# Five tables of steps, one for each engine, in place of one common order in a decoder layer's last third

## The chip, the cores and the metric

The kernel runs on one core of one Trainium2 chip. The metric is the device time of one execution in microseconds (us), as the median of several executions. The core has five instruction queues that run side by side: TensorE (PE, matrix products), VectorE (DVE), ScalarE (ACT), GpSimd (POOL) and SyncE (SP, which here only starts transfers). Each queue is worked off strictly in the order in which it was written; between queues there are only semaphores.

## The reference

One pre-norm decoder layer over 16 sequences of 128 tokens with 256 channels. Three residual blocks follow each other:

```python
# latent attention, 16 heads, latent width 72, causal
Wdkv = x @ latent_w + latent_b
q = jnp.einsum('btc,hcl->bhtl', x, Wd_w) + Wd_b[None, :, None, :]
scores = jnp.einsum('bhtl,bsl->bhts', q, Wdkv) / jnp.asarray(np.sqrt(d_head), dtype=x.dtype)
attn = jax.nn.softmax(jnp.where(causal, scores, -jnp.inf), axis=-1)
y = jnp.einsum('bhts,bsl->bhtl', attn, Wdkv)
z @ out_w + out_b
# bidirectional RWKV with the context as key and value, gate from x
jax.nn.sigmoid(r) * (Af + Ab + cur * v) / (Bf + Bb + cur)
# mixture of experts: 8 experts, 2 for each token
h = jax.nn.silu(x @ w_gate[e].T) * (x @ w_up[e].T)
out = out + dense_w[:, e:e + 1] * (h @ w_down[e].T)
x = x + attn(layernorm(x)); x = x + xattn(layernorm(x), ctx, ctx); x = x + ffn(layernorm(x))
```

## The kernel before

**Two halves.** The first half, to about 361 us, is attention and RWKV. Attention is cut into 64 units (one sequence, four heads each). The second half is the expert stage. Each token is written into a list of its two experts, and the lists are cut into tiles: 16 big tiles (0 to 15) of 256 rows and 7 small ones (16 to 22) of 128 rows. Tiles 0 to 4 are planned from the first 12 sequences (groups 0 to 2 of four sequences) before attention ends; all others wait for the last group's routing (`phase(j)` is 1 from tile 5 on).

**The names of the steps**, as the tables have them. A unit n of attention is `S.n` (scores on PE L727 and L731, their maximum on DVE L1197, exponentials on ACT L983), `N.n` (reciprocal DVE L1201, scaling POOL L1593), `T.n` (transposition PE L739, copy ACT L988), `Y.n` (mixing PE L748, copy DVE L1212, packing by four transfers on SP L574). `O.b.i` is quarter i of sequence b's output projection (PE L776, for sequence 15 L761), `add` adds two sequences' results to x.

For a group's second and third normalisation and routing there are `bn`, `agg`, `rs` (POOL L1588), `nmb`, `xn` (ACT L950), `tx` (transpositions PE L686, copies ACT L961), `lg` (router scores PE L792), `r1` and `r2` (the two choices, DVE L1294 to L1306, and exponentials on ACT L1032), `r3` (ranks, PE L799 and L803, slots on DVE L1321 to L1325), `rw` (weights, DVE to L1332), `r4` (eight scatters of token numbers into the lists, POOL L1636), and `p1`, `p2`, `p3` (which expert and which rows each tile has, some 40 short DVE instructions, L1340 to L1435).

A tile j of the expert stage goes through:

- `ltk.j`: its token numbers TK, loaded by SP at L631 or L633 (tiles 0 to 2: `gtk`, POOL L1668). Tiles from 5 on wait for `p3` of the last group and for its scatters.
- `lxg.j`: rows gathered by POOL (L1650, two instructions in a big tile, one in a small one) into one of four buffers; gather j waits until PE has transposed tile j-4.
- `lw.j.k`: weights of 512 KB for gate, up and down (k = 0, 1, 2), SP L620 and, for the small tiles, L604 (tile 0: `gw`, POOL L1660). Each waits until the block that lay there before has been split.
- `sw.j.k`: that block split into two parts, ACT L1048 and then DVE L1132 (big tiles only).
- `tg.j`: rows transposed (PE L818, ACT L1056 or L1054, DVE L1132).
- `up.j.n`: half n of the gate and up products (PE L668 with outputs P; a small tile has one, L852), then `si` (Silu, ACT L1062), `hd` (product, DVE L1463 or L1456) and `sh` (split, ACT L1069 and DVE L1132).
- `dn.j`: the down product (PE L668 with outputs PO, 24 matmuls; in a small tile L861, 8), then a copy with the weight (`weigh`, ACT L1077) into Y, one of two buffers.
- `ao.j`: POOL adds Y to the output rows in HBM (L1677). It waits until the additions of `ao.j-1` have landed. `weigh` of tile j waits until those of `ao.j-2` have landed.

```python
po.wait_ge(s_acc, 16 * parts_before(j))        # add_out, ahead of L1677
ac.wait_ge(s_acc, 16 * parts_before(j - 1))    # weigh, ahead of L1077
```

**What sets the order.** `schedule()` makes one list ORDER of 1060 steps: the text STEPS, and from tile 10 on a loop. Every engine walks this same list and emits its own part of each step. So a step that is late in the list is late on all five queues. The semaphore counts are also taken from ORDER (`nth`, `before`).

Of the kernel before, what the change touches and what calls it, by code (L numbers as in the profile page):

```python
# [1770 lines left out]
```

## Time and profile before

| | us |
| --- | --- |
| median of 3 executions | 604.07 |
| the three | 602.4, 604.07, 605.44 |
| the profiled execution | 600.46 |
| its span, first to last instruction | 598.8 |
| PE busy | 520.2 (87%) |
| VectorE, ScalarE, GpSimd busy | 362.9, 329.9, 314.7 |

All rows are of the one profiled execution, whose own time is 600.46 us: its span and 1.7 us around it. It lies 3.6 us under the median. Times of rows count from the start of the span.

### The profile page before, as it was taken

To read this page: it belongs to the slowest core of one execution; us is meant where nothing else is said; L and a number is where in the kernel's file an instruction comes from. 1 tells how busy PE (TensorE), PEld (TensorE's weight loads), DVE (VectorE), ACT (ScalarE), POOL (GpSimd) and SP (SyncE) were. 2 spreads that over 40 slices of the span, in tenths; PEclk is the share of its full clock that TensorE was granted. 3 is DMA by queue.
4 is the path that set the end of the run, shared out by engine and by line. 5 is a ranking of instruction groups with operands and counts; after the bars stand their busy time and mean duration, and the time that the engine had idled before them with its cause. 6 is when DMAs were issued, how large, how long until landed. Compare 5 with 4: busy or idle time off the path is not lost.

```text
span 598.8 us, 10336 instructions
## 1 busy us (share of the span) xinstructions
PE 520.2 (87%) x3448; PEld 453.2 (76%) x3448; DVE 362.9 (61%) x740; ACT 329.9 (55%) x945; POOL 314.7 (53%) x277
## 2 busy tenths in 40 slices
...
DMA packets 53219, 76.82 MB, mean 128 GB/s; under 512 B 10173, under 2 KB 41662, under 8 KB 52838
## 3 DMA queue, kind: packets, MB, share of 16 engines
...
q10 hardware_dynamic: 804, 0.15, 0.1%
...
## 4 chain that ended last, share of the span: by engine, by line
PE 58%; DVE 9%; issue 9%; POOL 9%; DMA 7%; ACT 5%; SPq 2%; POOLq 0%; DVEq 0%; ACTq 0%
PE P L668 18%; PE PO L776 7%; PE P L731 6%; PE P L748 6%; PE PO L668 5%; PE P L739 3%; PE P L852 3%; POOL EB L1593 2%; DMA cxa<-xd,TK 2%; POOL cxa L1650 2%; ACT EB L983 2%; PE PO L861 2%; PE P L727 2%; PE P L686 1%; PE P L792 1%
## 5 line engine op out<-in xcount | busy, mean ns | idle before, releaser
L983 ACT ACTIVATE EB<-P,small 128x128 f32<-128x128 f32 x256 | 90.4, 369 | 74.7 <-DVE small L1197 64.6
L1593 POOL TENSOR_TENSOR EB<-EB,small 128x512 f32<-128x512 f32 x64 | 78.8, 1241 | 86.1 <-DVE small L1201 86.0
L668 PE MATMUL P<-GT,WF 128*128 128x256 f32 x768 | 101.9, 291 | 6.0 <-DVE GT L1132 2.6
L668 PEld LDWEIGHTS P<-GT,WF 128*128 128x128 f32 x768 | 97.4, 198 | 7.2 <-DVE GT L1132 3.1
L1677 POOL DMA_INDIRECT out<-Y,TK x39 | 65.8, 1687 | 65.2 <-DMA out<-Y,TK 29.2
L731 PEld LDWEIGHTS P<-KT,qT 72*128 72x128 f32 x512 | 69.8, 198 | 11.5 <-DMA qT<-qP 6.4
L748 PE MATMUL P<-PT,V 128*72 128x512 f32 x128 | 67.0, 605 | 9.7 <-ACT PT L988 8.2
L731 PE MATMUL P<-KT,qT 72*128 72x128 f32 x512 | 70.3, 282 | 5.1 <-DMA qT<-qP 5.1
L776 PE MATMUL PO<-Ow,zP 128*128 128x256 f32 x270 | 67.5, 390 | 2.7 <-DMA zP<-ZT 2.7
L1212 DVE COPY ZT<-P 72x512 f32<-72x512 f32 x64 | 43.3, 676 | 40.4 <-PE P L748 39.4
L776 PEld LDWEIGHTS PO<-Ow,zP 128*128 128x128 f32 x270 | 50.5, 195 | 15.9 <-issue 10.3
L1197 DVE TENSOR_REDUCE small<-P 128x4 f32<-128x512 f32 x64 | 43.3, 677 | 26.3 <-PE P L731 26.1
L1650 POOL DMA_INDIRECT cxa<-xd,TK x39 | 42.9, 1100 | 30.1 <-DMA TK<-xs 20.0
L668 PE MATMUL PO<-WF,HR 128*128 128x256 f32 x384 | 51.9, 294 | 4.5 <-issue 4.5
L988 ACT ACTIVATE PT<-P 128x512 f32<-128x512 f32 x64 | 38.8, 607 | 27.8 <-PE P L739 27.8
L668 PEld LDWEIGHTS PO<-WF,HR 128*128 128x128 f32 x384 | 49.9, 202 | 4.9 <-issue 4.9
L983 ACT ACTIVATION_READ_ACCUMULATOR EB<-P,small 128x1 f32 x256 | 52.9, 207 | 0.0
L1636 POOL DMA_INDIRECT xs<-TKS,SL x32 | 33.7, 1052 | 35.9 <-DVE TKS L1332 25.6
L739 PEld LDWEIGHTS P<-ident,EB 128*128 128x128 f32 x256 | 31.4, 144 | 22.1 <-issue 10.7
L739 PE MATMUL P<-ident,EB 128*128 128x128 f32 x256 | 39.9, 279 | 4.6 <-POOL EB L1593 4.5
L1077 ACT ACTIVATE Y<-PO,TK 128x256 f32<-128x256 f32 x39 | 16.7, 470 | 38.9 <-DMA out<-Y,TK 15.0
L976 ACT ACTIVATE qP<-P,small 128x256 f32<-128x256 f32 x72 | 30.9, 483 | 12.4 <-PE P L668 12.3
...
## 6 DMA issues: line engine op xcount, KB each, us to landing
...
```

Source lines behind the costliest of these rows:

```text
L668: r = e.matmul(o, lt(a), rt_(b), start=start and n == 0, stop=stop and n == 2, skip_group_check=skip)
L731: p = e.matmul(S[:, 128 * j:128 * j + 128], qT[k % 2][:, 4 * hq + j, c:c + 128], KT[g % 2][:, r:r + 128], start=False, stop=True, skip_gro ...
L739: p = e.transpose(PTB[:, 128 * j:128 * j + 128], EB[n % 3][:, j, :], ident[:, :])
L748: e.matmul(YB[0:L, :], V[g % 2][:, b % GB, :], PT[n % 2][:, :], start=True, stop=True).then_inc(s_Y, 1)
L776: p = e.matmul(o, zP[b // NB % 2][:, m, 128 * (b % NB):128 * (b % NB) + 128], Ow[:, m, :], start=m == 0, stop=m == NQ - 1)
L983: e.activation(EB[i][:, j, :], S[:, 128 * j:128 * j + 128], ACT.Exp, bias=NM[i][:, j:j + 1], accum_out=SM[i][:, j:j + 1]).then_inc(s_exp, 1)
L988: e.activation(PT[n % 2][:, :], PTB[:, :], ACT.Copy).then_inc(s_pt, 1)
L1197: e.tensor_reduce(NM[n % 3], SB[n % 2][:, :].rearrange("p (h s) -> p h s", h=4), AX.X, ALU.max, negate=True).then_inc(s_max, 1)
L1212: e.tensor_copy(ZT[buf][:, :, c:c + 128], YB[0:L, :].rearrange("p (h t) -> p h t", h=4)).then_inc(s_z, 1)
L1593: e.tensor_tensor(EB[i][:, :, :], EB[i][:, :, :], SM[i].unsqueeze(2).broadcast_to([128, 4, 128]), ALU.mult).then_inc(s_prob, 1)
L1650: e.indirect_dma_start(XG[i][:, a_, :], None, xd[0:(TN * 3 // 4, TN + 1)[phase(j)], :], bass.IndirectOffsetOnAxis(ap=TK[:, j, a_, 0:1].bit ...
L1677: e.indirect_dma_start(outr, bass.IndirectOffsetOnAxis(ap=TK[:, j, a_, 0:1].bitcast(i32), axis=0), Y[j % 2][:, a_, :], None, bounds_check= ...
```

## The change

Each engine gets a text of its own with its own steps: SYNC_STEPS, TENSOR_STEPS, VECTOR_STEPS, SCALAR_STEPS and GPSIMD_STEPS. ORDER remains, but only for counting semaphores. No instruction's work, tile or buffer changes. Up to the scores of unit 53 every engine's steps stand as before. From there on (VectorE from unit 54, PE and ScalarE from 55, SP from the store of group 2's rows) they stand in another order, which differs from engine to engine.

```diff
+SYNC_STEPS = """
...
+    lw.11.0 lw.10.2 lw.12.1 lw.12.0 lw.13.1 lw.13.0 lw.11.2 lw.14.1 ltk.18 lw.12.2 lw.14.0 ltk.19 ltk.20 lw.13.2 lw.14.2 lw.15.1 lw.17.1 ltk.21 ltk.22
+    lw.15.0 lw.17.0 lw.16.0 lw.16.1 lw.15.2 lw.16.2 lw.18.0 lw.17.2 lw.18.1 lw.19.1 lw.18.2 lw.19.2 lw.19.0 lw.20.0 lw.20.2 lw.20.1 lw.21.2 lw.21.1
...
+def steps_of(table):
+
+    return [(name, *map(int, a)) for name, *a in (w.split(".") for w in table.split())]
+
+
 def schedule():
 
-    order = [(name, *map(int, a)) for name, *a in (w.split(".") for w in STEPS.split())]
+    order = steps_of(STEPS)
...
-            for name, *a in ORDER:
+            for name, *a in steps_of(SYNC_STEPS):
...
-            for name, *a in ORDER:
+            for name, *a in steps_of(TENSOR_STEPS):
...
-            for name, *a in ORDER:
+            for name, *a in steps_of(SCALAR_STEPS):
...
-                ve_.wait_ge(s_xb, i + 1)
+                ve_.wait_ge(s_xb, nth("xb", i))
...
-            for s in ORDER:
+            for s in steps_of(VECTOR_STEPS):
...
-            for s in ORDER:
+            for s in steps_of(GPSIMD_STEPS):
```

The line on `s_xb` lets the first additions to x wait for the bias of their own sequences, which POOL adds in the order 2, 3, 0, 1.

**Place 1: TensorE and ScalarE around the last group's routing.** P0 to P3 take the gate and up products, P5 router scores and ranks, GT and WF are the split rows and weights of a tile (buffer 0 for even tiles). TensorE before, from the first half of tile 0 to tile 1:

```order
L668 MATMUL P0<-GT0,WF0 128x256 x12
L668 MATMUL P2<-GT0,WF0 128x256 x12
L686 MATMUL P5<-ident,XN 128x128 x4
L792 MATMUL P5<-small,XT3 128x8 x8
L799 MATMUL P5<-Mr,Utr 128x32
L803 MATMUL P5<-Mr,onem 128x8 x10
L668 MATMUL P1<-GT0,WF0 128x256 x12
L668 MATMUL P3<-GT0,WF0 128x256 x12
L818 MATMUL P4<-ident,cxa 128x128 x4
L668 MATMUL PO<-WF0,HR0 128x256 x24
L668 MATMUL P0<-GT1,WF1 128x256 x12
```

and now:

```order
L894 MATMUL P5<-small,XT3 128x8 x8
L770 MATMUL P1<-GT0,WF0 128x256 x12
L770 MATMUL P3<-GT0,WF0 128x256 x12
L901 MATMUL P5<-Mr,Utr 128x32
L905 MATMUL P5<-Mr,onem 128x8 x10
L770 MATMUL P0<-GT1,WF1 128x256 x12
L770 MATMUL P2<-GT1,WF1 128x256 x12
L770 MATMUL P1<-GT1,WF1 128x256 x12
L770 MATMUL P3<-GT1,WF1 128x256 x12
L920 MATMUL P4<-ident,cxa 128x128 x4
L770 MATMUL PO<-WF0,HR0 128x256 x24
```

The second half of tile 0 stands between scores and ranks, and all of tile 1's products stand ahead of tile 0's down product. ScalarE before, around the exponentials of the routing (L1032) and the first Silu (L1062):

```order
L961 ACTIVATE XT3<-P5 128x256 x2
L1032 ACTIVATE small<-small 128x64
L1062 ACT_TABLE_LOAD
L1062 ACTIVATE SG0<-P0 128x512
L1062 ACTIVATE SG1<-P1 128x512
L1069 ACTIVATE HR0<-HF0 128x512
```

and now:

```order
L1164 ACT_TABLE_LOAD
L1164 ACTIVATE SG0<-P0 128x512
L1164 ACTIVATE SG1<-P1 128x512
L1171 ACTIVATE HR0<-HF0 128x512
L1158 ACTIVATE GT0<-P4 128x512
L1171 ACTIVATE HR0<-HF1 128x512
L1134 ACT_TABLE_LOAD
L1134 ACTIVATE small<-small 128x64
L1150 ACTIVATE WF0<-arena 128x1024
L1164 ACT_TABLE_LOAD
```

The exponentials moved behind two Silu, which gives two more table loads.

**Place 2: GpSimd after the last group's scatters.** cxa is where rows are gathered to, xs the lists, Y0 and Y1 hold results for even and odd tiles. Before:

```order
L1650 DMA cxa<-xd,TK 128x256 x2
L1636 DMA xs<-TKS,SL 18432x2 x4
L1677 DMA out<-Y0,TK 2048x256 x2
L1677 DMA out<-Y1,TK 2048x256 x2
L1650 DMA cxa<-xd,TK 128x256 x6
L1677 DMA out<-Y0,TK 2048x256 x2
L1650 DMA cxa<-xd,TK 128x256 x2
L1677 DMA out<-Y1,TK 2048x256 x2
L1650 DMA cxa<-xd,TK 128x256 x4
L1677 DMA out<-Y0,TK 2048x256 x2
```

and now:

```order
L1738 DMA xs<-TKS,SL 18432x2 x8
L1752 DMA cxa<-xd,TK 128x256 x6
L1779 DMA out<-Y0,TK 2048x256 x2
L1752 DMA cxa<-xd,TK 128x256 x6
L1779 DMA out<-Y1,TK 2048x256 x2
L1779 DMA out<-Y0,TK 2048x256 x2
L1752 DMA cxa<-xd,TK 128x256 x2
L1779 DMA out<-Y1,TK 2048x256 x2
L1752 DMA cxa<-xd,TK 128x256 x2
L1779 DMA out<-Y0,TK 2048x256 x2
```

The gathers of tiles 4 to 6 moved ahead of the first addition to the output, and those of tiles 7 to 9 ahead of the second.

**Place 3: SyncE near the end.** TK takes a tile's token numbers, WS1 and WS2 the weights of small tiles 20 and 21. Before, around tile 19's numbers:

```order
L604 DMA WS1<-wf 128x1024
L629 TENSOR_LOAD PI
L629 ISA x2
L633 ISA
L633 DMA TK<-xs 128x2
L603 TENSOR_LOAD PI
L603 ISA x2
L604 ISA
L604 DMA WS2<-wf 128x1024
```

and now, with arena holding tile 14's gate weights:

```order
L722 DMA arena<-wf 128x1024
L731 TENSOR_LOAD PI
L731 ISA x2
L735 ISA
L735 DMA TK<-xs 128x2
L731 TENSOR_LOAD PI
L731 ISA x2
L735 ISA
L735 DMA TK<-xs 128x2
```

The numbers of the small tiles now stand ahead of the weights of tile 15 and of all weights that wait for the down products.

## Rows read from the trace of the kernel before

**Rows 1.** Stretches: us, busy of PE, PEld, DVE, ACT, POOL, granted clock, DMA share, GB/s.
```profile
340.00:397.00 57.00, 42.83 (x186) 35.35 (x187) 27.35 (x74) 19.30 (x31) 23.03 (x24) 0.68 0.45 132
463.00:536.00 73.00, 73.00 (x606) 73.00 (x606) 52.15 (x63) 49.58 (x79) 39.25 (x29) 0.99 0.89 238
```

**Rows 2.** Timeline of PE: start, us, line, count, idle before it and what ended it.
```profile
375.16 3.58 PE L792 MATMUL P<-small,XT 128*128 128x8 f32 x16 [0.47 <-ACT XT L961]
382.16 0.40 PE L799 MATMUL P<-Mr,Utr 128*128 128x32 f32 x1 [3.42 <-DVE small L1306]
...
384.52 5.42 PE L668 MATMUL P<-GT,WF 128*128 128x256 f32 x24
...
392.23 4.61 PE L668 MATMUL PO<-WF,HR 128*128 128x256 f32 x24 [1.85 <-issue]
...
403.23 6.36 PE L668 MATMUL P<-GT,WF 128*128 128x256 f32 x48
...
460.16 4.43 PE L668 MATMUL PO<-WF,HR 128*128 128x256 f32 x24 [2.63 <-issue]
...
558.11 0.69 PE L818 MATMUL P<-ident,cxa 128*128 128x128 f32 x2 [5.22 <-DMA cxa<-xd,TK]
558.59 3.62 PE L861 MATMUL PO<-arena,HS 128*128 128x256 f32 x8
562.00 4.61 PE L852 MATMUL P<-GS,WS 128*128 128x128 f32 x32
...
566.67 1.89 PE L861 MATMUL PO<-WR,HS 128*128 128x256 f32 x8
568.40 3.73 PE L852 MATMUL P<-GS,WS 128*128 128x128 f32 x32
```

**Rows 3.** Timeline of ScalarE: the table load ahead of Silu, and a held copy into Y.
```profile
382.41 1.28 ACT L1062 ACT_TABLE_LOAD   x1
...
457.98 0.84 ACT L1077 ACTIVATE Y<-PO,TK 128x256 f32<-128x256 f32 x2 [4.13 <-DMA out<-Y,TK]
```

**Rows 4.** Timeline of VectorE: end of the routing, one and the last of the plan.
```profile
387.36 0.20 DVE L1332 RECIPROCAL TKS<-small 128x8 f32<-128x8 f32 x1
...
409.01 0.17 DVE L1416 TENSOR_TENSOR small<-small 1x18 f32<-1x18 f32 x1
...
416.00 0.16 DVE L1435 CAST PI<-small 1x18 int32<-1x18 f32 x1
```

**Rows 5.** Timeline of GpSimd: first scatter, then first instruction of `ao` 0, 2 to 5, 15, 22.
```profile
388.42 1.05 POOL L1636 DMA_INDIRECT xs<-TKS,SL  x1 [16.95 <-DVE TKS L1332]
...
403.14 1.62 POOL L1677 DMA_INDIRECT out<-Y,TK  x1 [0.30 <-issue]
...
430.18 1.86 POOL L1677 DMA_INDIRECT out<-Y,TK  x1 [0.30 <-issue]
...
446.13 2.65 POOL L1677 DMA_INDIRECT out<-Y,TK  x1 [0.30 <-issue]
...
458.75 1.61 POOL L1677 DMA_INDIRECT out<-Y,TK  x1 [2.98 <-ACT Y L1077]
...
465.29 1.55 POOL L1677 DMA_INDIRECT out<-Y,TK  x1 [3.03 <-ACT Y L1077]
...
555.18 1.57 POOL L1677 DMA_INDIRECT out<-Y,TK  x1 [1.56 <-ACT Y L1077]
...
589.72 1.55 POOL L1677 DMA_INDIRECT out<-Y,TK  x1 [1.98 <-DMA out<-Y,TK]
```

**Rows 6.** Waits from 340 to 600: waiter <- releaser: us in total, times, longest.
```profile
POOL out L1677 <- DMA out<-Y,TK: 29.2, 10, 5.1
```

**Rows 7.** Timeline of SP: numbers of tile 5; numbers of tile 19, weights behind them.
```profile
416.96 0.34 SPq L631 DMA_DIRECT2D TK<-xs  x1
...
544.87 0.34 SPq L633 DMA_DIRECT2D TK<-xs  x1
545.99 5.88 SPq L604 DMA_DIRECT2D WS<-wf  x6
```

More of the change, by code:

```diff
@@ L182 @@
 """
+SYNC_STEPS = """
+    ctx.0 q.0.0 q.0.1 q.0.2 q.0.3 q.0.4 q.1.0 ctx.1 q.1.1 q.1.2 q.1.3 Y.1 q.1.4 Y.3 q.2.0 Y.5 q.2.1 q.2.2 Y.7 ctx.2 q.2.3 Y.9 q.2.4 Y.11 q.3.0 Y.13
+    q.3.1 q.3.2 Y.15 q.3.3 Y.17 ctx.3 q.3.4 Y.19 q.4.0 Y.21 q.4.1 Y.23 q.4.2 q.4.3 Y.25 q.4.4 out.0.0.4 Y.27 xd.0.0.4 q.5.0 Y.29 q.5.1 Y.31 q.5.2 Y.33
+    q.5.3 q.5.4 Y.35 q.6.0 Y.37 q.6.1 Y.39 q.6.2 Y.40 q.6.3 Y.41 out.1.0.4 Y.42 q.6.4 Y.43 Y.44 xd.1.0.4 q.7.0 Y.45 q.7.1 Y.46 Y.47 q.7.2 Y.48 q.7.3
+    Y.49 Y.50 q.7.4 Y.51 Y.52 Y.53 Y.54 Y.55 Y.56 owh Y.57 Y.58 ltk.3 Y.59 xd.2.0.4 lw.1.1 lw.1.2 xd.3.0.2 lw.2.0 lw.1.0 out.2.0.4 ltk.4 lw.2.2 lw.2.1
+    lw.3.2 lw.3.1 out.3.0.2 xd.3.2.2 lw.3.0 lw.4.0 lw.4.1 out.3.2.2 ltk.5 lw.5.0 lw.5.1 ltk.6 ltk.7 ltk.8 lw.6.0 ltk.9 ltk.10 lw.4.2 lw.6.1 lw.5.2
+    lw.7.1 lw.8.1 ltk.11 ltk.12 ltk.13 lw.7.0 lw.8.0 ltk.14 lw.9.0 lw.6.2 lw.9.1 ltk.15 ltk.16 lw.7.2 lw.8.2 lw.9.2 lw.10.1 lw.11.1 ltk.17 lw.10.0
+    lw.11.0 lw.10.2 lw.12.1 lw.12.0 lw.13.1 lw.13.0 lw.11.2 lw.14.1 ltk.18 lw.12.2 lw.14.0 ltk.19 ltk.20 lw.13.2 lw.14.2 lw.15.1 lw.17.1 ltk.21 ltk.22
+    lw.15.0 lw.17.0 lw.16.0 lw.16.1 lw.15.2 lw.16.2 lw.18.0 lw.17.2 lw.18.1 lw.19.1 lw.18.2 lw.19.2 lw.19.0 lw.20.0 lw.20.2 lw.20.1 lw.21.2 lw.21.1
+    lw.22.1 lw.21.0 lw.22.0 lw.22.2
@@ new lines @@
+"""
+VECTOR_STEPS = """
+    bn.1.0.0.0 bn.1.0.0.2 agg.1.0.0.4 nmb.1.0.0.4 split tx.1.0.0.4.0 tx.1.0.0.4.1 consts bn.1.1.0.0 bn.1.1.0.2 vb.0 w1.0.0 agg.1.1.0.4 S.0 S.1
+    nmb.1.1.0.4 w2.0.0 N.0 N.1 w3.0.0 S.2 w4.0.0 w5.0.0 tx.1.1.0.4.0 w1.0.1 N.2 S.3 Y.0 tx.1.1.0.4.1 S.4 w8.0.0.0 w2.0.1 Y.1 N.3 w3.0.1 w4.0.1 S.5
+    w5.0.1 N.4 Y.2 N.5 S.6 w8.0.0.1 w8.0.0.2 Y.3 w8.0.0.3 w1.1.0 S.7 Y.4 S.8 N.6 N.7 S.9 bn.1.2.0.0 Y.5 w8.0.1.0 bn.1.2.0.2 S.10 Y.6 N.8 w2.1.0 w3.1.0
+    Y.7 N.9 agg.1.2.0.4 S.11 bn.1.3.0.0 vb.1 bn.1.3.0.2 S.12 Y.8 N.10 N.11 w4.1.0 w5.1.0 agg.1.3.0.4 w8.0.1.1 w8.0.1.2 w1.1.1 Y.9 N.12 S.13 w8.0.1.3
+    S.14 Y.10 N.13 S.15 Y.11 w8.1.0.0 N.14 N.15 Y.12 w2.1.1 S.16 nmb.1.2.0.4 w3.1.1 w4.1.1 w5.1.1 Y.13 S.17 w8.1.0.1 N.16 Y.14 w8.1.0.2 w8.1.0.3
+    w1.2.0 S.18 N.17 S.19 N.18 Y.15 Y.16 add.0 w8.1.1.0 tx.1.2.0.4.0 N.19 w2.2.0 S.20 Y.17 S.21 w3.2.0 w4.2.0 N.20 N.21 tx.1.2.0.4.1 S.22 w5.2.0 Y.18
+    w1.2.1 w8.1.1.1 N.22 Y.19 w8.1.1.2 w8.1.1.3 S.23 vb.2 Y.20 S.24 Y.21 N.23 S.25 w8.2.0.0 S.26 N.24 Y.22 w2.2.1 w3.2.1 w4.2.1 w5.2.1 N.25 N.26 add.1
+    S.27 Y.23 bn.2.0.0.0 bn.2.0.0.2 agg.2.0.0.4 N.27 Y.24 w1.3.0 nr.0.0.4 w8.2.0.1 S.28 Y.25 w8.2.0.2 x2.0.0.0.0 w8.2.0.3 S.29 N.28 Y.26 x2.0.0.2.0
+    N.29 S.30 bn.3.0.0.0 bn.3.0.0.2 agg.3.0.0.4 Y.27 S.31 nmb.3.0.0.4 w8.2.1.0 Y.28 S.32 N.30 w2.3.0 Y.29 N.31 N.32 w3.3.0 S.33 w4.3.0 w5.3.0 w1.3.1
+    Y.30 w8.2.1.1 w8.2.1.2 S.34 w8.2.1.3 Y.31 lgc.0.0.4 N.33 N.34 S.35 r1.0.0.4 r2.0.0.4 ra.0.0.4 add.2 nmb.1.3.0.4 N.35 Y.32 S.36 r3.0.0.4 rw.0.0.4
+    Y.33 N.36 S.37 Y.34 tx.1.3.0.4.0 S.38 w8.3.0.0 N.37 N.38 tx.1.3.0.4.1 Y.35 w2.3.1 w3.3.1 w8.3.0.1 S.39 w8.3.0.2 Y.36 S.40 w4.3.1 N.39 N.40 Y.37
+    S.41 bn.2.1.0.0 S.42 Y.38 S.43 Y.39 w5.3.1 N.41 w8.3.0.3 N.42 add.3 bn.2.1.0.2 agg.2.1.0.4 Y.40 vb.3 N.43 S.44 nr.1.0.4 x2.1.0.0.0 x2.1.0.2.0 Y.41
+    S.45 N.44 bn.3.1.0.0 bn.3.1.0.2 S.46 N.45 Y.42 agg.3.1.0.4 Y.43 nmb.3.1.0.4 S.47 N.46 w8.3.1.0 Y.44 S.48 add.4 N.47 N.48 w8.3.1.1 w8.3.1.2
+    w8.3.1.3 Y.45 S.49 Y.46 lgc.1.0.4 N.49 r1.1.0.4 Y.47 S.50 r2.1.0.4 S.51 ra.1.0.4 r3.1.0.4 rw.1.0.4 S.52 Y.48 N.50 Y.49 N.51 N.52 add.5 bn.2.2.0.0
+    S.53 Y.50 N.53 S.54 bn.2.2.0.2 agg.2.2.0.4 N.54 Y.51 Y.52 nr.2.0.4 x2.2.0.0.0 S.55 S.56 x2.2.0.2.0 Y.53 bn.3.2.0.0 bn.3.2.0.2 N.55 N.56
+    agg.3.2.0.4 nmb.3.2.0.4 S.57 S.58 Y.54 Y.55 Y.56 lgc.2.0.4 r1.2.0.4 S.59 r2.2.0.4 N.57 N.58 N.59 ra.2.0.4 S.60 r3.2.0.4 rw.2.0.4 p1.0 p2.0 S.61
+    S.62 Y.57 add.6 Y.58 N.60 N.61 p3.0 Y.59 N.62 bn.2.3.0.0 agg.2.3.0.2 nr.3.0.2 Y.60 S.63 x2.3.0.0.1 Y.61 bn.3.3.0.0 N.63 sw.0.0 agg.3.3.0.2
+    nmb.3.3.0.2 sw.0.1 Y.62 Y.63 sw.0.2 add.7 bn.2.3.2.0 agg.2.3.2.2 nr.3.2.2 tg.0 x2.3.2.2.1 bn.3.3.2.0 agg.3.3.2.2 nmb.3.3.2.2 sw.1.2 tg.1 sw.1.1
+    sw.1.0 hd.0.0 lgc.3.0.4 r1.3.0.4 r2.3.0.4 hd.0.1 sh.0.0 tg.2 r3.3.0.4 ra.3.0.4 sh.0.1 rw.3.0.4 p1.1 p2.1 hd.1.0 sw.2.0 sw.2.1 tg.3 hd.1.1 sh.1.0
+    sw.3.0 sh.1.1 p3.1 hd.2.0 sw.3.1 hd.2.1 sw.2.2 sw.4.0 sh.2.0 sh.2.1 tg.4 sw.4.1 hd.3.0 hd.3.1 sh.3.0 tg.5 hd.4.0 sh.3.1 sw.3.2 sw.5.1 sw.5.0
+    hd.4.1 sw.6.1 sh.4.0 sw.6.0 sh.4.1 tg.6 hd.5.0 hd.5.1 sw.4.2 sh.5.0 sw.7.0 sw.5.2 sh.5.1 tg.7 sw.7.1 hd.6.0 hd.6.1 sw.6.2 sh.6.0 sh.6.1 tg.8
+    sw.8.0 sw.8.1 sw.9.1 hd.7.0 hd.7.1 sw.7.2 sh.7.0 sw.8.2 sh.7.1 hd.8.0 tg.9 sw.9.0 hd.8.1 sh.8.0 tg.10 sw.10.1 sw.10.0 sh.8.1 hd.9.0 hd.9.1 sw.9.2
+    sh.9.0 sw.10.2 tg.11 sw.11.1 sh.9.1 sw.11.0 hd.10.0 sw.12.1 hd.10.1 sh.10.0 sh.10.1 hd.11.0 sw.12.0 tg.12 hd.11.1 sw.11.2 sh.11.0 sh.11.1 hd.12.0
+    tg.13 sw.12.2 sw.13.0 sw.13.1 sw.14.1 hd.12.1 sh.12.0 sh.12.1 hd.13.0 hd.13.1 sh.13.0 tg.14 sw.14.0 sw.13.2 tg.15 sh.13.1 hd.14.0 hd.14.1 sw.15.0
+    sw.15.1 sw.14.2 sh.14.0 sh.14.1 sw.15.2 hd.15.0 hd.15.1 sh.15.0 hd.16.0 sh.15.1 hd.17.0 hd.18.0 hd.19.0 hd.20.0 hd.21.0 hd.22.0
```

53 lines of the change are left out of this document (added).

## The prediction, made before the changed kernel ran

> **What bounds the kernel now.** I first read the stretches. From 463 to 536 us PE is busy all the time at full clock [rows 1], so there no order gains anything. From 340 to 397, where attention ends and the expert stage starts, PE is busy 42.8 of 57 us at a granted clock of 0.68 [rows 1], which is a mix of both levels, 1.2 and 2.4 GHz. Then I read PE's own timeline for holes, and the queues of GpSimd and SyncE for what ended them. Three places stand out: the routing of the last group (3.42 and 1.85 us idle), a hole of 2.63 us ahead of the down product at 460.16, and one of 5.22 us at 558.11 [rows 2]. Behind each the same work takes longer: 24 matmuls 5.42 us at 384.52, 48 of them 6.36 us at 403.23 [rows 2].
>
> Last I looked at what runs beside PE. The additions into the output are a chain of their own: `ao.j` waits until `ao.j-1` has landed, and 29.2 us of GpSimd's waits are on that [rows 6]. From `ao.4` at 458.75 to `ao.15` at 555.18 they start every (555.18 - 458.75) / 11 = 8.77 us [rows 5]. PE's own pace for a tile is two halves and a down product: 6.36 + 3 us (24 of 48 matmuls) [rows 2], close to 9.1 with the overlap of rows. So PE and this chain run at nearly the same pace, and a gain of PE counts only as far as the chain begins earlier too. This is what decides my number.
>
> **The change part by part.** Up to unit 53 nothing moves. Between there and the end of attention steps are exchanged both ways. GpSimd issues group 2's eight scatters in one go, ahead of the scaling of unit 60 (pitch about 1.3 us, as the first scatter lasts 1.05 us [rows 5], so some 10 us), ScalarE splits tile 0's weights ahead of the copy of unit 62. The first delays, the second has those weights ready when tile 0 starts. I walked both orders and take the sum as 0, with 4 us either way.
>
> *Routing (place 1).* Take the scores at 375.16 as before. They end at 378.7. The second half of tile 0 now fills the wait of 3.42 us and ends at 378.7 + 5.4 = 384.1; ranks take 382.16 to 384.52 = 2.4 us [rows 2], to 386.5. Then two halves, a transposition and the down product, 6.4 + 0.4 + 3 us at full clock: PE could start tile 2 at 396.3. What is late next is VectorE: it had finished the routing at 387.56 [rows 4], now 2 us later because the ranks are 2 us later (386.5 for 384.5), and then has `p1` and `p2`, 29 instructions of some 0.2 us (the one of L1416 lasts 0.17 [rows 4], and each waits for the one before), 5.8 us, then a product of 0.6 us and a split of 1.2 us. That is 397. Tile 2 started at 403.23 [rows 2]: **6.2 us** gained. If the clock stays low for all of it, 24 matmuls cost 5.4 for 3.1 us three times more, and 3 us are left of it; if it is full from the scores on, it is some 10.
>
> *Table loads.* The exponentials of the routing now follow two Silu, which adds two loads of 1.28 us [rows 3], 2.6 us on ScalarE. They lie beside VectorE's 5.8 us of planning, so I cost them at nothing; without that cover they would cost 2.6. The Trainium skill speaks against this edit (ScalarE: Activation LUTs, What ACT_TABLE_LOAD costs): a switch of sets costs 1.28 us and a drain of 1.38. The trace has the first number and shows no drain of that size. With it the two would take 5.3 us, by that page's figures an estimate, still just under the cover.
>
> *Middle.* The hole at 460.16 came from a copy into Y that waited 4.13 us for `ao.3` to land [rows 3], and held the split behind it on ScalarE. `ao.3` had started late, at 446.13 [rows 5], because it stood behind a gather whose token numbers were late. The plan now ends earlier: `p3` follows 5.8 + 6.6 + 2.8 us (planning, eight short steps of tiles 1 to 3 and 14 instructions) after 389.5, at about 405, for 416.16 [rows 4]; SyncE's load of tile 5's numbers at 416.96 [rows 7] moves with it. Gain on PE 2.63 + (4.43 - 3.1) = **4.0 us** [rows 2], bounds 0 and 5.
>
> *Tail (place 3).* Tile 19's numbers are issued at 544.87, behind six weight transfers at 538.10 and with six behind [rows 7]; its gather is what PE waits 5.22 us for, and the clock falls. Now these numbers are loaded some 20 us earlier. Gain 5.22 + (3.62 - 1.89) + (4.61 - 3.73) = **7.8 us** [rows 2]. Tile 20's products now stand ahead of tile 17's down product, which costs nothing, as products and results have two buffers each. The weights behind are still issued only after the down products 14 and 15; they have 15 us of PE work ahead of them, so nothing is late next.
>
> PE alone: 6.2 + 4.0 + 7.8 = 18.0 us.
>
> *The cap (place 2).* `ao.0` now stands behind the gathers of tiles 5 and 6, which need the whole plan. `p3` at 405, numbers issued 0.8 us later (416.16 to 416.96 [rows 4, 7]) and landed some 2 us after that (assumed), two gathers of 2.6 us, between them tile 6's numbers, which stand behind a weight block that waits for tile 3's split: `ao.0` starts at about 413.5 for 403.14 [rows 5]. But then the chain has no hole left: at 8.8 us each `ao.2` starts at 431 (430.18 before), `ao.3` at 440 (446.13), `ao.4` at 449 (458.75), `ao.15` at 413.5 + 15 x 8.8 = 545.5 for 555.18 [rows 5]. That is 9.7 us. The last seven take 589.72 - 555.18 = 34.5 us [rows 5]; some of them waited for Y, so I give them 1.3 us. Sum **11 us**, less than PE's 18, so it decides.
>
> Profiled execution: 600.46 - 11.0 = 589.5 us. It lies 3.6 us under the median, so I forecast 604.07 - 11.0 = **593.0 us**.
>
> **The rivals.**
>
> 1. *The chain gives way.* Where less is in flight, `ao.4` to `ao.5` took 465.29 - 458.75 = 6.5 us [rows 5]. At 8.3 or less the chain is never behind PE, and all 18 to 20 us show: 604.07 - 19 = 585. For it: its pace before may be PE's own. Against: 29.2 us of waits on landed additions [rows 6].
> 2. *Attention's end loses what routing gains.* The scatters hold unit 60 by some 3 us, a copy of unit 62 waits for weights, the clock drops earlier. Then tile 2 starts no earlier than 403, `ao.0` at 420, and 4 us are left: 600.
> 3. *Slower.* The additions start later and the DMA engines are fuller (share 0.89 already [rows 1]), since weights and gathers now come in a shorter time. `ao.3` to `ao.4` took 12.6 us [rows 5]. If the chain starts at 413.5 and its first five go at 12.6 instead of 8.8, `ao.15` comes at 564.5, 9 us later than before: 613. It decides from a mean pace of (555.18 - 413.5) / 15 = 9.45 us, or a start after 423.
> 4. *Nothing.* What the order frees, another wait takes at once, since both paces are the same: 603 to 605.
>
> **How the numbers follow.** Forecast 0.55; rival 1 0.15; rival 2 0.12; rival 3 0.10; rival 4 0.08. A measurement of this kernel can tell about 0.5%, 3 us. Forecast and rival 1 are faster, rival 2 mostly so: faster 0.79, same 0.10, slower 0.11. The range leaves out most of rival 3 and the far half of rival 1: 584 to 603.
>
> **What would show it.** In the changed profile: PE's hole at the ranks gone and tile 2 at 397; `p3` done at 405; no hole of PE at a gather of tiles 19 to 22; and `ao.0` at 413, then a start every 8.8 us up to `ao.15` at 545, with PE waiting for copies into Y in the last third. If PE has no holes there but additions come every 8.3 us, rival 1 is right. If PE waits for scaled units between 334 and 340, it is rival 2. I am wrong altogether if weights arrive later than their splits, for SyncE now loads them in another order (tile 8's up block ahead of tile 7's gate block), which I followed only by what each waits for.

## The result, and the profile after

The changed kernel is slower. It was timed twice, each time beside the old one on the same chip:

| | changed, us | old, us | ratio, 95% interval |
| --- | --- | --- | --- |
| first | 615.15 (4 executions, 611.97 to 616.86) | 604.44 (4) | 1.0195 (1.0143 to 1.0247) |
| second, `after_again` | 612.14 (6) | 600.07 (11) | 1.0231 (1.0171 to 1.0291) |

One of the six executions of the second timing, 636.18 us at a mean granted clock of 0.82 where the others have 0.94 to 0.95, was a slow one, and the ratio leaves it out.

The forecast was 593.0 in a range of 584 to 603, and faster. What was measured lies outside it and is a loss, of 1.4 to 2.9% over both intervals. Below, "the changed kernel" in figures of the chip of the experiments is 600.7 x 1.0195 = 612.4. With the second ratio it would be 614.6, so each difference that is counted from it below is uncertain by some 2 us.

Two executions of the changed kernel are profiled: 616.86 us (first) and 608.47 us (second). In the first, unit 20 of attention already starts 4.2 us later than in the old kernel's profile (132.4 for 128.2), though nothing stands in another order there. That is a difference between executions, and the second does not have it (126.7). So I read the second, and give the first beside it where it matters. Lines of the changed file are 102 higher: L1677 is now L1779, L1077 is L1179, L668 is L770.

The stretches, with the columns of [rows 1]:

```profile
340.00:397.00 57.00, 48.52 (x290) 42.67 (x289) 38.12 (x112) 30.24 (x51) 27.75 (x28) 0.87 0.57 171
...
463.00:536.00 73.00, 66.01 (x513) 65.50 (x514) 44.41 (x55) 40.91 (x67) 40.19 (x27) 0.90 0.73 197
```

From 340 to 397 PE does more than before (48.52 us busy for 42.83) at a clock of 0.87 for 0.68: the routing gained. But from 463 to 536, where PE had been busy for all of its 73 us, it is now busy for 66, and the DMA share fell from 0.89 to 0.73. PE's timeline, where [rows 2] has the routing and the hole at 460.16:

```profile
374.44 1.95 PE L894 MATMUL P<-small,XT 128*128 128x8 f32 x16
376.25 3.11 PE L770 MATMUL P<-GT,WF 128*128 128x256 f32 x24
380.31 0.28 PE L901 MATMUL P<-Mr,Utr 128*128 128x32 f32 x1 [0.95 <-DVE small L1408]
...
392.20 5.92 PE L770 MATMUL P<-GT,WF 128*128 128x256 f32 x48
...
464.44 5.46 PE L770 MATMUL PO<-WF,HR 128*128 128x256 f32 x24 [8.32 <-issue]
```

The second half of tile 0 now stands ahead of the ranks and takes 3.11 us (5.42 before), the hole ahead of them shrank from 3.42 to 0.95 us, and tile 2 starts at 392.20 (403.23 before). Then, at tile 7's down product, PE is idle for 8.32 us (456.12 to 464.44). ScalarE's timeline tells why:

```profile
462.25 0.84 ACT L1179 ACTIVATE Y<-PO,TK 128x256 f32<-128x256 f32 x2 [8.37 <-DMA out<-Y,TK]
462.98 0.63 ACT L1171 ACTIVATE HR<-HF 128x512 fp32r<-128x512 f32 x1
```

The copy of tile 6 into Y waits 8.37 us until `ao.4` has landed, and behind it on ScalarE stands the split that tile 7's down product needs. PE is ahead of the additions, and is held until they catch up. GpSimd's timeline from `ao.0` to `ao.1`, the gathers of tiles 5 and 6 ahead of it:

```profile
404.42 1.62 POOL L1752 DMA_INDIRECT cxa<-xd,TK  x1 [4.51 <-DMA TK<-xs]
...
410.68 0.95 POOL L1752 DMA_INDIRECT cxa<-xd,TK  x1 [2.98 <-DMA TK<-xs]
411.93 0.95 POOL L1752 DMA_INDIRECT cxa<-xd,TK  x1 [0.30 <-issue]
413.18 1.87 POOL L1779 DMA_INDIRECT out<-Y,TK  x1 [0.30 <-issue]
415.36 1.58 POOL L1779 DMA_INDIRECT out<-Y,TK  x1 [0.30 <-issue]
417.25 1.03 POOL L1752 DMA_INDIRECT cxa<-xd,TK  x1 [0.30 <-issue]
...
425.99 0.95 POOL L1752 DMA_INDIRECT cxa<-xd,TK  x1 [0.30 <-issue]
427.24 1.62 POOL L1779 DMA_INDIRECT out<-Y,TK  x1 [0.30 <-issue]
```

`ao.0` starts at 413.18, where the forecast had it (413.5). But `ao.1` starts only at 427.24. `ao.0` had landed at 420.4, and six gathers of tiles 7 to 9 stand between (417.25 to 426.94). The waits from 340 to 600, where [rows 6] showed 29.2 us on landings:

```profile
POOL out L1779 <- ACT Y L1179: 48.1, 13, 7.4
ACT Y L1179 <- DMA out<-Y,TK: 43.4, 11, 8.4
POOL out L1779 <- DMA out<-Y,TK: 27.8, 7, 5.9
```

The second line was 15.0 us in 4 waits before: ScalarE now waits for landings too, 43.4 us of it. Most of the first line is the same wait: 12 of the 15 additions `ao.1` to `ao.15` start 0.8 to 1.0 us behind the landing of the one before, also where the profile names the copy into Y, which the same landing had released.

**The account of the chain.** The additions are strictly one behind the other, so the start of the last one, `ao.22`, is a sum: start of `ao.0`, the sixteen times from a big tile's first addition to its landing, the holes (time from a landing to the next start; a single hole is given whole, in sums each of the fifteen counts without the 0.9 us that it takes when all is ready), and the last seven. With 0.9 us for each of the sixteen steps from a landing to the next start, 14.4 us in all, a row adds up to its `ao.22`. Landings are read from the trace's DMA records.

| profiled execution | `ao.0` | 16 landings | holes | `ao.16` to `ao.22` | `ao.22` | holes over 2 us, ahead of |
| --- | --- | --- | --- | --- | --- | --- |
| before | 403.1 | 127.7 | 17.7 | 26.7 | 589.7 | 1, 2, 3 |
| after, first | 422.0 | 128.7 | 16.8 | 24.2 | 606.1 | 1, 7, 9 |
| after, second | 413.2 | 128.2 | 17.7 | 24.1 | 597.6 | 1, 7, 9 |

From `ao.22` to the end of the span it is 9.1 or 9.2 us in all three. The old kernel's 17.7 us of holes lay ahead of `ao.1` to `ao.3`, the new one's lie elsewhere and are as large. What differs is the start: 10.1 us later (18.9 in the first), less 2.6 in the last seven. That is the 7.9 us (16.4) between the profiled executions. So the account puts both kernels' end on this one chain, and the experiments have to show it.

### The profile page after: what moved, and what is told of

It reads as the page before. It is cut to its first block, busy times and chain, and to the rows that moved or that the text cites. A ratio compares the mean times of both kernels' runs of the same rounds, so it can differ in the third digit from the quotient of the medians.

```text
span 615.2 us, 10358 instructions
## 1 busy us (share of the span) xinstructions
PE 523.5 (85%) x3448; PEld 456.2 (74%) x3448; DVE 361.9 (59%) x740; ACT 331.8 (54%) x947; POOL 319.0 (52%) x277
## 4 chain that ended last, share of the span: by engine, by line
PE 41%; DMA 16%; issue 13%; POOL 13%; DVE 8%; ACT 6%; POOLq 1%; SPq 1%; another core or an unknown queue 0%; ACTq 0%; DVEq 0%
PE P L770 12%; DMA out<-Y,TK 12%; PE PO L878 6%; PE P L833 6%; PE P L850 5%; POOL xs L1738 4%; PE P L841 3%; POOL EB L1695 3%; PE PO L770 3%; POOL cxa L1752 2%; POOL out L1779 2%; ACT EB L1085 2%; PE P L829 1%; DMA qT<-qP 1%; DMA arena<-wd 1%
## 5 line engine op out<-in xcount | busy, mean ns | idle before, releaser
L770 PE MATMUL P<-GT,WF 128*128 128x256 f32 x768 | 102.6, 295 | 7.1 <-DVE HF L1565 3.5
L1779 POOL DMA_INDIRECT out<-Y,TK x39 | 65.2, 1672 | 81.2 <-ACT Y L1179 42.8
L770 PEld LDWEIGHTS P<-GT,WF 128*128 128x128 f32 x768 | 99.3, 203 | 8.3 <-DVE GT L1234 5.3
L833 PEld LDWEIGHTS P<-KT,qT 72*128 72x128 f32 x512 | 72.4, 204 | 11.3 <-DMA qT<-qP 6.0
L850 PE MATMUL P<-PT,V 128*72 128x512 f32 x128 | 67.9, 612 | 10.9 <-ACT PT L1090 7.4
L833 PE MATMUL P<-KT,qT 72*128 72x128 f32 x512 | 72.6, 288 | 5.1 <-DMA qT<-qP 5.1
L1752 POOL DMA_INDIRECT cxa<-xd,TK x39 | 47.4, 1215 | 20.2 <-issue 11.2
L770 PE MATMUL PO<-WF,HR 128*128 128x256 f32 x384 | 51.4, 293 | 6.7 <-issue 6.7
L770 PEld LDWEIGHTS PO<-WF,HR 128*128 128x128 f32 x384 | 49.3, 200 | 6.9 <-issue 6.9
L841 PEld LDWEIGHTS P<-ident,EB 128*128 128x128 f32 x256 | 32.2, 148 | 29.2 <-issue 20.1
L841 PE MATMUL P<-ident,EB 128*128 128x128 f32 x256 | 41.2, 286 | 10.4 <-issue 3.9
L1179 ACT ACTIVATE Y<-PO,TK 128x256 f32<-128x256 f32 x39 | 16.6, 470 | 39.9 <-DMA out<-Y,TK 39.9
```

Source lines behind the costliest of these rows:

```text
L770: r = e.matmul(o, lt(a), rt_(b), start=start and n == 0, stop=stop and n == 2, skip_group_check=skip)
L833: p = e.matmul(S[:, 128 * j:128 * j + 128], qT[k % 2][:, 4 * hq + j, c:c + 128], KT[g % 2][:, r:r + 128], start=False, stop=True, skip_gro ...
L841: p = e.transpose(PTB[:, 128 * j:128 * j + 128], EB[n % 3][:, j, :], ident[:, :])
L850: e.matmul(YB[0:L, :], V[g % 2][:, b % GB, :], PT[n % 2][:, :], start=True, stop=True).then_inc(s_Y, 1)
L1752: e.indirect_dma_start(XG[i][:, a_, :], None, xd[0:(TN * 3 // 4, TN + 1)[phase(j)], :], bass.IndirectOffsetOnAxis(ap=TK[:, j, a_, 0:1].bit ...
L1779: e.indirect_dma_start(outr, bass.IndirectOffsetOnAxis(ap=TK[:, j, a_, 0:1].bitcast(i32), axis=0), Y[j % 2][:, a_, :], None, bounds_check= ...
```

## The experiments

Each is compared with runs of the old kernel on the same chip. Of long lines of tables the diffs show only the part that bears on the point. h2, b, c, c2, d and f are written in the changed file, with the old order in its tables, so that their lines are 102 higher too. My theory (A) is that the serial chain of additions sets the end, and that the new order starts it late and breaks it. The rivals: the new end of attention is the loss (B), or the new order costs PE or VectorE time of its own (C, D). The changed kernel itself ran once more, with the result above:

> The new kernel itself once more, beside the two below on one chip, since its loss was measured with four executions only and all repairs are counted from it. From the first measurement: 1.4 to 2.5% slower than the old one, 610 to 616 us.

### Which half of the change: h1_attn_old, h2_experts_old

Each engine's table was cut at `tg.0`, the first step of the expert stage, and one part put back. GpSimd's part ahead of it, as an example:

```diff
-    N.56 N.57 N.58 N.59 r4.2.0.4.0.0 r4.2.0.4.0.2 r4.2.0.4.1.0 r4.2.0.4.1.2 N.60 N.61 gtk.0
+    N.56 N.57 N.58 r4.1.0.4.1.2 N.59 N.60 r4.2.0.4.0.0 r4.2.0.4.0.2 r4.2.0.4.1.0 N.61
```

> The new kernel, with every engine's steps up to the end of attention (up to tg.0) in the old order, the expert stage in the new one. Theory A (the late and broken chain of output additions is the loss, attention's end adds some 4.5 us): about 615 - 4.5 = 610.5 us; the first addition ao.0 starts within 5 us of 422 - 4.5 = 417.5 in its trace. Theory B (the end of attention is the whole loss, everything behind is only shifted): the expert stage's gain shows, 604 - 7 = 597 us. Theory C (the expert stage's new order is the loss, and attention's end nothing): 615.

> The new kernel, with every engine's steps from tg.0 on in the old order and attention's end in the new one. Theory A: 604 + 4.5 = 609 us, ao.0 some 4 to 5 us later than in the kernel before (about 408), later additions with it. Theory B (attention's end is the whole loss): 615. Theory C: 604.

`h1_attn_old`: 610.08, ratio 1.014 (1.0095 to 1.0185). `h2_experts_old`: 601.07, ratio 0.9982 (0.9945 to 1.0019). In front of the old expert stage, the new order of attention's end costs nothing that can be measured. My expectation of 4.5 us for it came from the first profiled execution alone and was wrong, and that the 610.5 us for `h1_attn_old` came true was luck. The loss is in the expert stage's tables: `ao.0` at 416.5 in `h1_attn_old`, at 406.8 in `h2_experts_old`. Rival B falls. `h1_attn_old` lies 3 to 5 us under the changed kernel with intervals that overlap, so a small cost of attention's end together with the new tables is not excluded.

### Is it the chain: after_half_add, before_half_add

```diff
-                for a_ in range(parts_of(j)):
+                for a_ in range(1):
```

with the counts of landings waited for changed to match.

> The new kernel with only the first 128 rows of each tile's result added into the output (the second addition of the 16 big tiles is left out), so that each link of the chain of additions is shorter. Theory A: PE's gain from the routing and the tail becomes visible, and this kernel is as fast as or faster than the old one with the same cut, by up to 18 - 4.5 = 13 us (by at least 5 us). Theory D (the new order costs PE or VectorE time of its own, whatever the additions do): it stays some 10 us behind the old one with the same cut.

> The old kernel with the same cut: only the first 128 rows of each tile's result are added. Theory A: the old order has PE and the chain at nearly the same pace, so that it gains some 5 to 10 us, to 594 to 599. Theory D (additions bound nothing): within 3 us of 604.

New order: 588.66, ratio 0.9777 (0.9708 to 0.9846). Old order: 593.8, ratio 0.9881 (0.9797 to 0.9964). With full additions the new order is 11 to 14 us behind, with half of them 5.1 us ahead. The two intervals overlap, so that this lead is uncertain by some 6 us and not quite shown, but the swing of over 15 us is. Rival D falls, as it had the new order stay some 10 us behind: what the new order loses, it loses to the additions. From a tile's first addition to its landing it takes 5.8 us in the mean in both, for 8.0. From 463 to 536 PE is busy all the time again in the new order:

```profile
463.00:536.00 73.00, 73.00 (x616) 72.99 (x615) 49.00 (x61) 46.10 (x76) 30.03 (x23) 1.00 0.82 240
```

### Repairs of the new order: a1_start_early, a2_holes_closed, a12_both, g_ao0_only

a1, on GpSimd; on ScalarE the copies `dn.1` to `dn.4` move up likewise:

```diff
-    lxg.4 lxg.5 lxg.6 ao.0 lxg.7 lxg.8 lxg.9 ao.1 ao.2 lxg.10 ao.3
+    lxg.4 ao.0 lxg.5 ao.1 lxg.6 lxg.7 ao.2 lxg.8 lxg.9 ao.3 lxg.10
```

a2, on GpSimd, and on ScalarE (`dn.8` to `dn.11` likewise):

```diff
-    ao.6 lxg.12 lxg.13 ao.7 ao.8 lxg.14 lxg.15 lxg.16 lxg.17 ao.9 ao.10 lxg.18
+    ao.6 lxg.12 ao.7 lxg.13 ao.8 lxg.14 ao.9 lxg.15 ao.10 lxg.16 lxg.17 lxg.18
-    si.8.1 tg.10 sw.9.2 si.9.0 sh.8.1 sw.10.0 sw.11.0 sh.9.0 si.9.1 tg.11 sw.10.2 sh.9.1 dn.7
+    si.8.1 dn.7 tg.10 sw.9.2 si.9.0 sh.8.1 sw.10.0 sw.11.0 sh.9.0 si.9.1 tg.11 sw.10.2 dn.8 sh.9.1
```

a12 is both. g moves `ao.0` alone, ahead of `lxg.5`.

> The new kernel with the start of the chain of additions moved earlier: on GpSimd ao.0, ao.1, ao.2 and ao.3 each stand ahead of the gathers they stood behind (ao.0 ahead of the gather of tile 5, ao.1 ahead of 6, ao.2 ahead of 8, ao.3 ahead of 10), on ScalarE the copies dn.1 to dn.4 stand right behind where TensorE ends them. Theory A (the chain of additions sets the end, and it starts late): ao.0 at some 409 instead of 422, ao.5 bound by TensorE's down product 5 at some 457 instead of 473, and 12 to 16 us less than the new kernel: 598 to 603. Theory B2 (the holes at ao.7 and ao.9 take the gain back, as they are set by ScalarE's and GpSimd's order and not by the start): 5 us or less, 608 to 612. Theory D (the additions bound nothing): 613 to 615.

> The new kernel with the two later holes of the chain closed and its start as it is: on GpSimd ao.7 ahead of the gather of tile 13, ao.9 ahead of that of 15, ao.10 ahead of 16; on ScalarE the copies dn.7 to dn.11 at the place where TensorE's down product ends. Theory A: the holes before ao.7 (7.5 us) and ao.9 (6.7 us) shrink to some 1 us each, 10 to 12 us less than the new kernel: 602 to 605. Theory D: 613 to 615.

> The new kernel with both repairs together: the chain's start of a1_start_early and the closed holes of a2_holes_closed; nothing else of the change is undone. Those two took 7 and 10 us off the new kernel (612.4 by the ratio, 600.7 for the old). Theory A (start and holes are links of one chain, so that their gains add): some 596 us, 4 to 5 less than the old kernel, so that the change's other parts are a gain. If TensorE's pace or another wait takes over (theory E): 600 or more.

> The new kernel with the place of ao.0 alone undone: it stands ahead of the gather of tile 5. ao.1 still stands behind the gathers of tiles 7 to 9. Theory A: ao.0 at some 410, ao.1 and all behind only 4 us earlier (a hole ahead of ao.1 takes the rest), so 4 us less than the new kernel: 607 to 610. If ao.0 alone is the cause: 12 us less, 600.

a1: 605.74, ratio 1.0072 (1.0034 to 1.011), by the ratio 7.4 us off the changed kernel's 612.4 where 12 to 16 were expected. `ao.0` started at 407.3, but holes of 8.8 and 5.5 us opened: ahead of `ao.4`, whose down product PE starts only at 443.88 and which stands behind a gather that waits for PE too (448.11, 4.60 us), and ahead of `ao.5`, whose copy into Y stands on ScalarE behind a split that waits for the next down product. The one ahead of `ao.9` stayed (6.4). a2: 602.84, ratio 1.0034 (0.9996 to 1.0072), 9.7 us off, near to the 10 to 12 expected; the holes fell from 17 or 18 to 4.3 us. Both: 600.12, ratio 0.9993 (0.9947 to 1.0038). That is level with the old kernel, and 12.1 us off, not the 17 of an exact sum: the 600 or more that the expectation gave for another wait taking over, and not theory A's 596. Their account: start 403.8, holes 9.0, but landings 134.5 us for 128.2. g: 607.91, in a spread of 597.12 to 615.75 over 4 executions that gives no ratio, so its time shows neither 4 nor 12 us. In its trace `ao.0` is at 405.8 and `ao.1` at 426.8, with a hole of 11.9 us between. The changed kernel's second profile has `ao.1` at 427.2, so behind the gathers of five tiles it came no earlier for the early `ao.0`.

### The late start in the old kernel: f_ao0_late

```diff
-    r4.3.0.4.1.2 ao.0 ao.1 lxg.5 lxg.6 lxg.7 ao.2
+    r4.3.0.4.1.2 lxg.5 lxg.6 ao.0 ao.1 lxg.7 ao.2
```

> The old kernel with one step of the new put in on GpSimd: ao.0, and with it ao.1, stand behind the gathers of tiles 5 and 6 instead of ahead of them. Theory A (the start of the chain is what counts): ao.0 at some 428 instead of 403, but the old kernel's holes ahead of ao.2 and ao.3 (17.8 us) take up most of it; ao.3 at 454 instead of 446, and 8 us more than the old kernel: 607 to 610. Theory D (the place of these two additions is of no account): 600 to 602.

608.59, ratio 1.0178 (1.0105 to 1.0252): 8.5 us by the medians from the place of two steps, as theory A had it.

```profile
427.68 1.40 POOL L1752 DMA_INDIRECT cxa<-xd,TK  x1 [4.13 <-DMA TK<-xs]
429.38 0.95 POOL L1752 DMA_INDIRECT cxa<-xd,TK  x1 [0.30 <-issue]
430.63 1.64 POOL L1779 DMA_INDIRECT out<-Y,TK  x1 [0.30 <-issue]
```

`ao.0` starts 27.5 us later than in the old kernel, the holes fall from 17.7 to 2.1 us, and the landings from 127.7 to 124.9. So a late start costs only what the holes behind it don't take up. PE finishes its last down product at 594.8 for 586.6: it follows the chain.

### Two terms of the sum alone: d_routing_only, b_tail_tokens

d takes the new order on PE up to `dn.2` and what belongs to it, and leaves GpSimd's additions; b only moves loads of token numbers on SyncE:

```diff
-    lw.14.2 ltk.16 lw.17.0 lw.17.1 lw.15.2 lw.16.0 lw.16.1 lw.16.2 ltk.17 lw.18.0 lw.18.1
+    lw.14.2 ltk.16 ltk.17 ltk.18 ltk.19 ltk.20 ltk.21 ltk.22 lw.17.0 lw.17.1 lw.15.2
```

> The old kernel with the new order of the last group's routing alone (TensorE to dn.2, VectorE to sw.4.1, ScalarE to si.3.1, SyncE to ltk.8); GpSimd's additions and gathers and everything behind stand as in the old one. The prediction's term for it is 6.2 us. Theory A (the chain of additions sets the end, and it still starts behind the same gathers): tile 2's first product at 395 to 397 instead of 403, but 0 to 3 us less than the old kernel at the end: 598 to 601. By the prediction's term alone: 594.5.

> The old kernel with one thing of the new: SyncE loads the token numbers of tiles 17 to 22 ahead of the weights of tile 17, some 20 us earlier. The prediction's term for this is 7.8 us of TensorE. Theory A: TensorE's hole of 5.22 us at tile 19 goes and its clock stays up, but the additions follow one another without a hole from ao.15 to ao.19 in the old kernel, and only the last three have some room (1.2 to 2.4 us each behind the landing): 1 to 2.5 us less than the old kernel. By the prediction's term alone: 7.8 us less.

d: 597.35, ratio 0.9969 (0.9924 to 1.0014): at most a few us, and not clear of nothing, for the term's 6.2. Tile 2 starts at 394.9 for 403.2, as forecast or better, but the additions move little: a hole of 9.1 us stands ahead of `ao.4`, behind gathers that wait for token numbers (444.81, 5.37 us). b: 601.15, ratio 1.0014 (0.9976 to 1.0053), nothing. PE still waits for gathers:

```profile
549.08 0.44 PE L920 MATMUL P<-ident,cxa 128*128 128x128 f32 x2 [4.01 <-DMA cxa<-xd,TK]
...
558.90 0.44 PE L920 MATMUL P<-ident,cxa 128*128 128x128 f32 x2 [2.40 <-DMA cxa<-xd,TK]
```

and GpSimd's timeline says why, the numbers being there long before:

```profile
549.07 1.57 POOL L1779 DMA_INDIRECT out<-Y,TK  x1 [6.35 <-ACT Y L1179]
550.95 1.56 POOL L1779 DMA_INDIRECT out<-Y,TK  x1 [0.31 <-issue]
552.81 1.01 POOL L1752 DMA_INDIRECT cxa<-xd,TK  x1 [0.30 <-issue]
```

Each gather stands behind an addition, and the addition behind an older landing. In the old kernel late numbers did hold the gather of tile 19, as GpSimd's timeline there shows:

```profile
552.62 1.00 POOL L1650 DMA_INDIRECT cxa<-xd,TK  x1 [3.99 <-DMA TK<-xs]
```

So the 5.22 us at 558.11 in [rows 2] were in large part theirs, as the prediction read it. With them early, PE waits 4.01 and 2.40 us behind the chain instead, and finishes its last down product at 587.3, for 586.6 before.

### What sets a landing: e_half_weights

```diff
+                if j > 5:
+                    b = (a + b) // 2
                 e.dma_start(WR[i][:, a:b], wf[bass.ds(v, 1), :, a:b].rearrange("a p n -> (a p) n")).then_inc(s_wf[i][k], 16)
```

> The old kernel, where from tile 6 on each weight block of the big tiles is loaded only to its first half (256 KB for 512 KB); all other steps stay. It asks what sets the time that an addition takes to land (some 8 us for 256 rows, where 128 rows at the quiet end land in 3). Theory F (it shares the DMA engines with the weights): ao.7 to ao.14 land in 5 to 6.5 us instead of 8.2, and 3 to 8 us less than the old kernel. Theory G (the additions' own reading and writing sets it): the landing stays at 8 us, and the time at 600 to 601.

594.33, ratio 0.9899 (0.9861 to 0.9936). In the profiled execution (593.0 us for 600.46) the sixteen landings sum to 119.1 us for 127.7, which is the gain. But it lies in `ao.0` to `ao.6`; those of `ao.7` to `ao.14` take 8.3 us in the mean, for 8.2. From 463 to 536 the traffic is 184 GB/s for 238 [rows 1], and they did not become shorter. So neither expectation held: the time fell as theory F had it, but its number for the later landings missed. That weights in flight lengthen the early landings is likely and rests on this one profile, and what sets the later ones stays open.

### A version that beats both: c_spliced, c2_spliced

c keeps attention's end and, from tile 3 or 4 on, everything as in the old kernel, takes the new routing between, loads the token numbers of tiles 17 to 22 early, and mostly alternates additions and gathers on GpSimd. c2 differs from c in this, and loads the token numbers of tiles 11 to 13 ahead of tile 9's weights:

```diff
-    lxg.4 ao.0 lxg.5 ao.1 lxg.6 lxg.7 ao.2 lxg.8 ao.3 lxg.9 ao.4 lxg.10 ao.5 lxg.11 ao.6 lxg.12 ao.7
+    lxg.4 ao.0 lxg.5 ao.1 lxg.6 lxg.7 ao.2 lxg.8 ao.3 lxg.9 ao.4 lxg.10 ao.5 ao.6 lxg.11 ao.7 lxg.12
```

> A version meant to beat both: the old order up to tg.0, then the new order through the routing (TensorE to dn.2, VectorE to sw.4.1, ScalarE to si.3.1 with the copy dn.1 ahead of sw.3.2, SyncE to ltk.8), then the old order again, with the token numbers of tiles 17 to 22 loaded early; GpSimd issues each addition ao.j as early as it can, with one gather between two additions. Theory A: ao.0 at some 404, ao.5 at 451 (bound by TensorE), then one every 8.9 us, the last at 575: 586 to 590 us, 12 to 15 less than the old kernel. If the new places of the additions only move the waiting to the gathers: 598 or more.

> c_spliced with its one hole closed: there ao.6 stood behind the gather of tile 11, which waited for token numbers until 467.5 us, and started 8.9 us after ao.5 had landed. Now the token numbers of tiles 11 to 13 are loaded ahead of the weights of tile 9, and from ao.6 on the gather of tile j+5 stands behind ao.j. Theory A: ao.6 at some 463 instead of 471, and 8 us less than c_spliced: 585 to 588. If TensorE's pace (9.1 us a tile) takes over: 3 to 5 us less, 589 to 592.

c: 598.05, ratio 0.9888 (0.9808 to 0.9968), where theory A had 586 to 590: its gather of tile 11 waited 9.54 us for token numbers ahead of `ao.6`. c2: 590.53, ratio 0.9834 (0.9771 to 0.9897). That is not theory A's 585 to 588 but the 589 to 592 given for PE's pace taking over, and from 463 to 536 PE is indeed busy for all of its 73 us. In the account of c2's profile the holes of the old kernel are gone (1.6 us left for 17.7), the start is at 407.4 (403.1) and the landings sum to 133.9 us (127.7), `ao.22` at 581.7 (589.7). `ao.0` itself now waits for something new:

```profile
407.42 2.22 POOL L1779 DMA_INDIRECT out<-Y,TK  x1 [3.90 <-DMA out<-X]
```

the store of the rows onto which it adds. Even here the largest share of the chain that ended last is landings; the page by line:

```profile
DMA out<-Y,TK 14%; PE P L770 8%; PE PO L878 7%; PE P L833 6%; PE P L850 6%; PE P L841 3%; POOL out L1779 2%; POOL EB L1695 2%; PE P L954 2%; ACT EB L1085 2%; PE P L829 2%; DMA cxa<-xd,TK 1%; DMA qT<-qP 1%; POOL xs L1738 1%; DVE small L1299 1%
```

## Why the prediction was wrong

**What bounds the kernel: right.** It named the chain of additions as the cap on PE's gain. The half additions show it: with them the same change is 5 us ahead (uncertain by 6) instead of over 10 behind.

**Attention's end, 0: right.** h2: 0.9982. The first profile pointed at a loss (last projection 370.6 for 361.8); about half of that was there from unit 20, and the second profile has none (360.6).

**Routing, 6.2 us: right in its mechanism, 1 to 3 us too small.** Tile 2 was forecast at 397 and started at 392.2 and 400.2 in the two profiles; measured from unit 53 of the same execution it came 9.5 and 7.3 us earlier. The second half of tile 0 took 3.11 us for the 5.4 put down for it, so the ranks, VectorE's end of the routing and the plan all came earlier: `p3` ended at 399.9 instead of the forecast 405. The lower bound of 3 us was summed wrongly, since three times 5.4 - 3.1 is 6.9 us and leaves nothing of the 6.2. Of the kernel's time the routing alone is worth 2 us or nothing (d).

**Table loads, 0: right.** They are there, and nothing waits. ScalarE's timeline:

```profile
381.53 1.28 ACT L1134 ACT_TABLE_LOAD   x1
382.82 0.26 ACT L1134 ACTIVATE small<-small 128x64 f32<-128x64 f32 x1
```

The next instruction starts 1.29 us after the load does. VectorE has work all that time, so neither load holds it. The Trainium skill (ScalarE: Activation LUTs, What ACT_TABLE_LOAD costs) adds a drain of 1.38 us to the 1.28; no such time stands in this trace, so the measurement decides.

**Middle, 4.0 us: the opposite came.** PE's hole ahead of a down product did not go, it grew from 2.63 to 8.32 us and moved to tile 7. The term took it to come from a late `ao.3` alone; it comes wherever PE is ahead of the additions, and the new order put PE further ahead. One more, of 5.51 us at 521.07, follows a copy into Y that is held for 7.86 us.

**Tail, 7.8 us: it was no gain of the kernel.** The late numbers were rightly read in the old trace, but behind them the chain holds the same gathers, so that the early numbers alone gave nothing (b). In the changed kernel, where the gathers also stand earlier on GpSimd, the last seven additions took 24.1 us for 26.7: 2.6 us. From `ao.15` to `ao.22` it was 30.7 for 34.5, 3.8 us where the forecast's sum had 1.3.

**The cap: here it failed, in the sentence "But then the chain has no hole left".** The start was forecast at 413.5 and measured at 413.2, which was luck in part: `p3` came 5 us earlier than forecast, and from there to `ao.0` it took 13.3 us for the 8.5 put down, as tile 5's numbers were issued 2.7 us after `p3` (402.57) for 0.8, and tile 6's only at 406.05, with their gather at 410.68. The first execution has 13.9 us there and starts at 422.0. No row stood behind the 2 us for the landing of the numbers; tile 5's gather starts 1.9 us after their issue. The pace was forecast at 8.8 and is (566.9 - 413.2) / 15 = 10.25 us. The difference at `ao.15`, 566.9 for 545.5, is 21.4 us: 17.7 of holes, the rest in landings of 8.2 us in the mean of the first fifteen (some 9.1 with the 0.9) for the 7.9 in 8.8. I had taken 8.8 from a stretch of the old kernel without holes, and had walked GpSimd's new order only as far as `ao.0`. The next rows of that order were enough to see it: three gathers (six instructions, 1.6 us each with their issue) ahead of `ao.1`, four ahead of `ao.9`, and on ScalarE `dn.7` behind a split that waits for tile 8's down product.

**The sign for being wrong altogether** was weights that arrive later than their splits. It showed: from 380 to 600 ScalarE waits 11.3 us, in five times, for weights, and never in the old kernel. It is not the loss, for with half additions it waits 10.9 us for them, and that kernel is faster than the old one.

**The rivals.** Rival 3 came true in its price (613) and its deciding point (a mean pace over 9.45), not in its mechanism: the DMA engines were less full than before (0.73), the chain was broken by other steps on its own two queues. It was given 0.10. Rival 2's "starts at 420 and 4 us are left" did not see that a start 17 us later uses up all 17.7 us of holes before anything can be gained. In f a start 27.5 us later left 2.1 us of them.

**Not settled.** Why two executions of one program start the chain at 413 and at 422 (5.7 of these 8.8 us are there from unit 20 on), and why landings sum to 125 us in f, 128 in the old kernel and both profiles of the changed one, 131 to 132 in h1 and a2, and 133 to 135 in a1, a12 and c2. An early start alone isn't it, as the old kernel starts earliest. With 16 landings these differences are as large as half a repair, and no run isolates them.
